# Waits of the gathers in a routed mixture-of-experts kernel: page pairs counted by VectorE instead of the most possible, with new step tables

## What is computed

```python
def body(acc, ws):
    ew1, ew2, ew3, ce = ws
    h = silu(xn @ ew1.T) * (xn @ ew3.T)
    return (acc + ce[:, None] * (h @ ew2.T), None)
...
y, _ = scan(body, zeros_like(xn), (w1, w2, w3, combine.T))
shared = silu(xn @ sw1.T) * (xn @ sw3.T) @ sw2.T
out = x + s * silu(y + shared)
```

## Time and profile before

| what | value |
| --- | --- |
| median of 3 runs | 708.12 us |
| the profiled execution: its own time | 709.27 us |
| the profiled execution: span from first to last instruction | 707.5 us |
| TensorE busy | 565.3 us, 80% |
| VectorE busy | 471.0 us, 67% |
| ScalarE busy | 370.3 us, 52% |
| GpSimd busy | 389.5 us, 55% |
| second part, first transpose to the end | 325.6 to 707.5 us |

### The profile page before, as it was taken

The page is one execution under the profiler, slowest core; times in us unless marked ns, Lnnn a source line. Parts: engine busy times, 40 slices in busy tenths (PEclk is TensorE's granted clock), DMA queues, the critical chain, the costliest instruction groups (busy, mean ns, idle before and its releaser), DMA issues.

```text
span 707.5 us, 14566 instructions
## 1 busy us (share of the span) xinstructions
PE 565.3 (80%) x4190; PEld 454.2 (64%) x4190; DVE 471.0 (67%) x1438; ACT 370.3 (52%) x618; POOL 389.5 (55%) x401
## 2 busy tenths in 40 slices
PE   8778878788694979535999988988888878888850
PEld 6556657475573766324999866767767767676730
DVE  7957888587785858911444466766766766676685
ACT  5536555355554464414776555655655646556441
POOL 1375667767675766761001555655655655565564
PEclk9879998979797979966999999999999999999985
DMA  9999995839392523585566889888888888888785
GB/s 322 409 358 349 365 316 195 300 120 357 139 334 94 208 83 120 193 104 190 165 206 198 256 275 284 278 275 276 265 293 291 269 269 276 274 268 276 231 252 150
DMA packets 100042, 174.81 MB, mean 247 GB/s; under 512 B 12290, under 2 KB 56066, under 8 KB 99074
## 3 DMA queue, kind: packets, MB, share of 16 engines
q1 hardware_dynamic: 76034, 108.29, 44.7%
q0 software_dynamic: 18432, 50.36, 23.1%
q10 hardware_dynamic: 5504, 15.24, 7.2%
HBM read 81.56 MB, written 92.27 MB: 246 GB/s over the span
## 4 chain that ended last, share of the span: by engine, by line
PE 57%; DVE 14%; issue 11%; ACT 8%; another core or an unknown queue 7%; DMA 2%; POOL 1%; ACTq 0%; SPq 0%; DVEq 0%; POOLq 0%
PE ps L787 23%; PE ps L807 10%; PE ps L775 8%; PE ps L689 5%; PE ps L673 4%; PE ps L797 4%; PE ps L695 2%; DVE sw L1070 1%; ACT w_all L524 1%; DVE w_all L990 1%; PE ps L661 1%; DVE stats L827 1%; PE ps L681 1%; ACT L546 1%
## 5 line engine op out<-in xcount | busy, mean ns | idle before, releaser
L474 POOL DMA_INDIRECT early<-slots_d,slot_at x192 | 187.6, 977 | 190.8 <-DMA slots_d<-early 65.1
L456 POOL DMA_INDIRECT slots_d<-early,slot_at x96 | 100.1, 1042 | 68.8 <-issue 25.7
L787 PE MATMUL ps<-w_all,xnT 128*128 x894 | 116.8, 273 | 15.4 <-issue 14.4
L456 POOL DMA_INDIRECT slots_d<-work,slot_at x96 | 99.7, 1038 | 49.7 <-issue 26.9
L1096 DVE CAST work<-ps 128x256 f16<-128x256 f32 x112 | 47.2, 422 | 113.7 <-remote 77.4
L787 PEld LDWEIGHTS ps<-w_all,xnT 128*128 128x128 f16 x894 | 80.1, 98 | 35.7 <-issue 26.4
L775 PE MATMUL ps<-ident,work 128*128 128x128 f16 x892 | 73.0, 221 | 27.4 <-issue 14.5
L807 PE MATMUL ps<-w_all,work 128*128 x669 | 92.6, 274 | 2.2 <-issue 2.2
L610 ACT ACTIVATE xnT<-ps 128x1024 f16<-128x1024 f16 x75 | 77.1, 1029 | 28.0 <-PE ps L775 14.0
L631 ACT ACTIVATE early<-ps 128x512 f32<-128x512 f32 x112 | 67.0, 599 | 43.7 <-PE ps L807 24.1
L616 ACT ACTIVATE work<-ps 128x256 f32<-128x256 f32 x112 | 43.9, 392 | 80.9 <-remote 57.9
(11 more groups left out here) (150 smaller groups left out, 889.4 us busy)
## 6 DMA issues: line engine op xcount, KB each, us to landing
work<-slots_d SPq DMA_DIRECT2D x112, 256.0 KB
slots_d<-early SPq DMA_DIRECT2D x112, 256.0 KB
slots_d<-pad SPq DMA_DIRECT2D x7, 3072.0 KB
w_all<-in_wexp ACTq DMA_DIRECT2D x7, 1536.0 KB
slots_d<-work SPq DMA_DIRECT2D x1, 5120.0 KB, 20.9
s_all<-in_x SPq DMA_DIRECT2D x8, 512.0 KB, 4.5
ysh_d<-work ACTq DMA_DIRECT2D x8, 512.0 KB
early<-ysh_d SPq DMA_DIRECT2D x32, 128.0 KB
```

Source lines behind the costliest of these rows:

```text
L456: pool.indirect_dma_start(slots_d[:, :], bass.IndirectOffsetOnAxis(ap=slot_at[:, at:at + 1], axis=0), split[b % XN_RING][:, t, :], None).t ...
L474: pool.indirect_dma_start(gath[:, at % GATH_RING, :], None, slots_d[:, :], bass.IndirectOffsetOnAxis(ap=slot_at[:, rank_of(at):rank_of(at) ...
L787: mm = pe.matmul(ps[:, 2 + p % 2, h * 2 * I:(h + 1) * 2 * I], xT[p % 3][:, x_low * HC + k, h * P:(h + 1) * P], w16[:, bass.ds(at + (w_low ...
```

## The change

The gathers' validity wait and the step tables change; no computation on the tokens does.

- VectorE gets two small instructions (`pairs_of_tiles`) after the page table: from `ends`, 32 int32 numbers `pairs_to[t] = (opened - 256) >> 8`, where `opened` is the number of slots opened up to the end of tile t. In pages n that is `n // 2 - 1`.
- GpSimd loads the 32 numbers into registers before its first gather. Before the gathers of rank 0 of tile t it waits until `pairs_of[t]` pairs have landed, before those of rank 3 for 2 more (`THIRD`). Tile 0 waits for constants. Ranks in between add no such wait.
- SyncE gets a stage `landed(p)`: it waits for the landing of store p, two steps behind its issue, and adds 1 to one semaphore, `s_landed`. GpSimd no longer waits for `s_store`.
- `in_steps` takes a table of steps for each stage. `sums`, `gate`, `load_shared`, `load_x_again` and `store_out` follow `SUMMED`: pair q of gathers is summed in step `23 + 29q // 30` instead of `26 + q`; the last, q = 95, in step 114 instead of 121.
- The pace: gather `at` waits for `due = 19 + 29at // 60` of `turn_hidden`, or `due + 2` of `hidden`, instead of 21 + at // 2 and 23 + at // 2.

```diff
-BEHIND = 4 * DEEP + 2
+SUMMED = [23 + q * 29 // 30 for q in range(GATHER_PAIRS)]
+THIRD = 2
+FIRST = 19
...
+            def landed(p):
+                sp.wait_ge(s_store[p % DEEP], p // DEEP * 16 + 16)
+                sp.sem_inc(s_landed, 1)
...
-            in_steps((load_slots, DEEP + 2, PAIRS), (store_y, -1 - LATE, PAIRS), (load_shared, -BEHIND + DEEP, GATHER_PAIRS),
-                     (load_x_again, -BEHIND, GATHER_PAIRS), (store_out, -BEHIND - DEEP, GATHER_PAIRS))
+            in_steps((load_slots, led(DEEP + 2, PAIRS)), (store_y, led(-1 - LATE, PAIRS)), (landed, led(-3 - LATE, PAIRS)),
+                     (load_shared, [s - DEEP for s in SUMMED]), (load_x_again, SUMMED),
+                     (store_out, [s + DEEP for s in SUMMED]))
...
-            stored = 0
+            pool.wait_ge(s_pairs_to, 1)
+            pairs_of = registers(nc, ENG.Pool, pairs_to, 0, TILES, PAIRS - THIRD)
             for at in range(GATHERS):
-                pages = at + E
-                complete = min(-(-pages // 2), PAIRS)
-                for pair in range(stored, complete):
-                    pool.wait_ge(s_store[pair % DEEP], 16 * (pair // DEEP + 1))
-                stored = complete
+                t, rank = at // TOP_K, at % TOP_K
+                if t == 0:
+                    pool.wait_ge(s_landed, -(-(E - TOP_K + 1 + rank) // 2))
+                elif rank == 0:
+                    pool.wait_ge(s_landed, pairs_of[t])
+                    pool.sem_inc(s_tile_in, 1)
+                elif rank == TOP_K // 2:
+                    pool.wait_ge(s_landed, pairs_of[t] + THIRD)
+                    pool.sem_inc(s_tile_in, 1)
                 if at >= GATH_RING:
                     pool.wait_ge(s_acc, at - GATH_RING + 1)
-                ahead = at // 2 + 18 + SOON
+                due = FIRST + at * 29 // 60
                 if at % 2 == 0:
-                    pool.wait_ge(s_eab_ps, min(ahead + 2, PAIRS))
+                    pool.wait_ge(s_eab_ps, min(due + 2, PAIRS))
                 else:
-                    pool.wait_ge(s_ehT_ps, min(ahead, PAIRS))
+                    pool.wait_ge(s_ehT_ps, min(due, PAIRS))
...
+            def pairs_of_tiles():
+                opened = ends[:, 1:1 + TILES * E].rearrange("p (t e) -> p t e", e=E)[:, :, E - 1]
+                then(dve.tensor_scalar(pairs_to[:], opened, -2.0 * P, None, ALU.add))
+                dve.tensor_scalar(pairs_to[:], pairs_to[:], 8, None, ALU.arith_shift_right).then_inc(s_pairs_to, 1)
...
-            in_steps((split_hidden, 0, PAIRS), (hidden_rows, SOON - 1, PAIRS), (sums, -BEHIND, GATHER_PAIRS))
+            in_steps((split_hidden, led(0, PAIRS)), (hidden_rows, led(SOON - 1, PAIRS)), (sums, SUMMED))
```

21 lines of the change are left out of this document (15 added, 6 removed).

## The result

The changed kernel takes 714.19 us (median of 20 runs, 705.81 to 718.32), the kernel before, timed beside it, 705.39 us (20 runs, 695.58 to 709.63). The ratio is 1.0142 with a 95% interval of 1.0109 to 1.0174; it is taken over the fast executions alone, those at most 1.5% above the fastest of their kernel, and so is not quite the quotient of the two medians (1.0125). The changed kernel is slower by 1.4%, inside the 2% band, where 702 us and a small gain were forecast. The profiled execution took 714.44 us, its span is 712.7. Lines have shifted: L616 is now L638, L1070 L1100, L474 L496, L1096 L1126, L775 L797, L787 L809, L797 L819, L807 L829.

What follows compares the result with a forecast made beforehand. The prediction took TensorE's steps, stretched by gathers, then VectorE's tail waiting for GpSimd's last gathers, as the bound. Terms of +3.6 and -10.1 us gave -6.5 us: 702 us forecast (-0.9%), range 692 to 711.

Steps and rivals of the forecast that it cites:

- The three stages: Second part: steps of 2.67 us before gathers, 3.33 us beside them, then a tail of 29.3 us from `split_hidden(108)`.
- the two counts: At `split_hidden(108)`: 187 gathers issued instead of 176, and 16 sums left for VectorE instead of 28.
- Terms 2 and 3: VectorE's work and idle time behind `split_hidden(108)`: stretch of 19.2 us instead of 29.3, a gain of 10.1 us.
- Terms 4 to 6: Instructions and register loads ahead of the loop, SyncE's store waits, GpSimd's changed waits: each forecast to cost nothing.
- term 1: 11 more gathers ahead of `split_hidden(108)`, at 0.33 us each, move that point by +3.6 us.
- No term rests on it: Claim that the granted clock, 0.60 of full on the mean in the tail, matters to no term.
- the two ends: Limits for the 11 moved gathers: 0 if free, 14.5 us if TensorE stood still through each whole gather, 1.32 us.
- GpSimd then makes up: After late data waits, at most 5.3 us, GpSimd catches up: one gather in 1.61 us needed, 1.32 possible.
- A: Rival: gathers moved ahead of TensorE's end are free, or the tail shortens more; -9.8 us, 698 us; chance 0.2.
- B: Rival: SyncE's landing waits hold up TensorE's loads, steps over 3.4 us; +16.5 us, 724.6 us; chance 0.07.
- C: Rival: last gathers come late, VectorE idles in the tail as before; sum about 0, 708 us; chance 0.15.
- D: Rival: VectorE's sums hold up GpSimd's gathers, binding at 1.7 us each; 715 us; chance 0.02.

Runs made afterwards that it cites:

- b_data_2: Changed kernel's data waits, registers and SyncE landing stage, but with the old step tables: 707.64 us, 1.0055 of the kernel before.
- b_train8_2: Kernel before, with GpSimd let go only at every eighth gather, same gathers in number and order: 820.78 us, ratio 1.1652.
- the last three runs: Half-step waits under another condition: changed kernel, two gathers a step from step 18 or 17, and kernel before: 605.02, 603.83, 612.19 us (0.989, 0.9882, 1.002).
- b_poolplain: Kernel before, with its 192 indirect gathers replaced by plain 128 KB loads issued by GpSimd behind the same waits: 642.10 us, ratio 0.9129.
- b_short: Kernel before, with each indirect gather cut to the first 64 of its 128 rows: 704.68 us, ratio 1.0.
- b_half_again: Kernel before, with even and odd gathers waiting for TensorE half a step apart, run under the other condition: 612.19 us, ratio 1.002.
- b_half: Kernel before, with even and odd gathers waiting for TensorE half a step apart, under the first condition: 702.29 us, ratio 0.997.

## Why the prediction was wrong

*What it had right.* The three stages, and the two counts: 187 gathers issued before `split_hidden(108)` and 16 sums left, as forecast. Terms 2 and 3 together said 19.2 us for the stretch behind that point, and it is 19.37. TensorE's last matmuls end 7.6 us before the span's end instead of 20.8. Terms 4 to 6, which had nothing for the registers, SyncE's waits and GpSimd's, were a little off: `b_data_2` measures them together at +0.55%, 3.9 us (1.6 to 6.2). Its trace has the same tail length as before within 1.3 us and runs of four like before's, and where the 3.9 us lie I can't say.

*The step that failed* is term 1: "11 more at 0.33 us: the point moves by +3.6 us". It moved by 15.1 us. The sum was +3.6 - 10.1; measured it is +15.1 - 9.9 = +5.2 us on the spans (712.7 - 707.5). The medians stand 8.8 us apart. Of the 15.1 us, 8.0 are more idle time of TensorE, 6.3 are its slower matmuls and 0.8 the earlier start of the second part. So the prediction's sentence on the clock, "No term rests on it", failed too: it had looked at the clock in the tail only. The price of 0.33 us was read correctly from the earlier trace rows and was an average over gathers that came in fours at a granted clock of 1.00. I took it for a property of a gather. `b_train8_2` shows that it is one of the pattern as well: the same gathers in eights cost 116 us more. The change alters the pattern: 2.07 gathers a step make a fifth in a row now and then, one late data wait is followed by a run of seven, and a run of seven comes about without one. How much of the 15.1 us is the pattern and how much the number of gathers is open, as said above. Of the two ends that I gave for the price, 0 and a whole gather (1.32 us, 14.5 us for the 11), the measured shift is at the upper one, and I had chosen by the nearest row.

*The sentence that hid a part of it* is in the part on the data wait: "GpSimd then makes up". The prediction found the places (gather 99 at tile 16, late by up to 5.3 us; measured 3.38, and 4.90 before gather 96) and asked only whether VectorE would stall. By the increments of `s_landed` the data wait comes last before seven gathers, 33, 66, 69, 96, 99, 126 and 129, which are at the tiles that the prediction named and at tile 11. VectorE doesn't stall: a sum starts 7.6 us or more after its gather. I did not ask what the catching-up does to the engine that shares nothing with it in the program.

*The rivals.* A (moved gathers are free): refuted here; it is what the last three runs show, where TensorE's step does not know of gathers. B (SyncE): refuted as a bound. TensorE, which SyncE's loads feed, waits for no load between 382 and 693 us; of 44.5 us of such waits 42.6 are "issue". The steps did become longer than 3.4 us (80 / 22 = 3.64), half of B's sign, for another reason. C (late last gathers): the last gather starts at 701.0 us, 2.4 us later than before, but only because all is shifted; VectorE idles 5.0 us in the tail instead of 8.0. D: a gather's middle length is 949 ns, unchanged. The Trainium skill, SBUF: State Buffer, section on who interferes with whom, has its lock for VectorE instructions in a two-port mode. No row shows whether the sums run in one, so the 949 ns don't test that rule; they show that these sums don't lengthen a gather. What was seen instead is TensorE held up beside GpSimd's gathers.

*How it does so* stays open. The runs show: only indirect transfers do it (`b_poolplain`), and as much with 64 rows as with 128 (`b_short`), TensorE works on for about 5 us and then gets its instructions singly (`b_train8_2`), and there is a condition without it (`b_half_again`). One could think that TensorE waits for a block of its instructions from memory. The trace speaks against the plain form of this. Queue q8 of the page moves 41 packets of the kind "instruction", 16 KB each; by their number, one to some 260 of TensorE's records, they are TensorE's. In the trace of after they start at 549.8 and 563.9 us, on either side of the starving at tile 16, and in `b_train8_2` at 496.2 and 513.7, on either side of the one shown. No experiment looked at TensorE's supply itself.

## What to carry to other kernels

A price per instruction that is read off a steady pattern holds for that pattern: before using it for moved instructions, look at how many will then follow each other without a gap, and whether the granted clock was full where it was read. In a kernel like this one, keep indirect gathers beside a busy TensorE in groups of four or fewer: eights cost 116 us here. Where gathers lie behind TensorE's end, try to start all of them earlier at the old pace rather than a few more in each step. In these runs that was no faster than before under the first condition (1.0002 at best) and 1% faster under the other.

## What the runs showed that I had not expected

- Replacing 192 indirect gathers by plain transfers of the same bytes, in the same queue, takes 9% off the kernel (704.70 to 642.10 us).
- GpSimd's gathers slow TensorE from 2.63 to 3.3 us a step with a granted clock of 1.00 in both; the profile calls this idle time "issue".
- The clock falls behind such starving: it stands at 0.96 in 500 to 580 us of after, 1.00 in the same stretch of before, and at 0.845 over the whole of `b_train8_2`. Nearly half of what the eights cost there is slower matmuls.
- The same kernel took 704.70 and 611.53 us on one chip at two times, with every gather as long as before. Part one, which scatters with the same form of instruction, was shorter too: the first pair of part two is reached at 292.5 us in `b_half_again`, at 327.7 in `b_half`.
- Gates half a step apart did not spread the gathers in `b_half`: they kept to fours, as before.
